# Key and query gammas folded into a second query weight, and a cross-attention kernel's opening laid out anew

## What is computed

```python
def _rms_norm(t, gamma):
    var = jnp.mean(jnp.square(t), axis=-1, keepdims=True)
    return t * jax.lax.rsqrt(var + EPS) * gamma
q = x @ Wq.T + bq                       # x: LayerNorm of x
kv = c @ Wkv.T + bkv                    # k and v interleaved
q = _rms_norm(q, q_gamma)
k = _rms_norm(k, k_gamma)
scores = jnp.einsum('bhnd,bhmd->bhnm', q, k) * scale
attn = jax.nn.softmax(scores, axis=-1)
out = jnp.einsum('bhnm,bhmd->bhnd', attn, v)
x = x + out
x = x + ffn(layernorm(x))               # 128 -> 512 -> 128, a piecewise-linear GELU, rounded to 1/256
```

## Time and profile before

| | us |
|---|---|
| median of 3 runs | 228.75 (228.58 to 230.69) |
| the profiled execution | 229.84 |
| its span, first to last instruction | 228.0 |
| PE busy (share of the span) | 181.1 (79%) |
| DVE busy | 190.6 (84%) |
| ACT busy | 146.7 (64%) |
| POOL busy | 129.8 (57%) |
| mean granted TensorE clock | 0.963 |

### The profile page before, as it was taken

One profiled execution on the slowest core, in us unless ns is written; L12 is line 12 of the kernel. 1 busy time (PEld: TensorE's weight loads), 2 busy tenths in 40 slices (PEclk: granted clock), 3 DMA queues, 4 the chain that ended last, 5 costly groups with the idle time before them and its releaser, 6 DMA issues.

```text
span 228.0 us, 8274 instructions
## 1 busy us (share of the span) xinstructions
PE 181.1 (79%) x3228; PEld 137.0 (60%) x3228; DVE 190.6 (84%) x347; ACT 146.7 (64%) x228; POOL 129.8 (57%) x175
## 2 busy tenths in 40 slices
PE   1168869888888888888898597865999999988664
PEld 0156648776676767667677455334666765665553
DVE  6878895988987888878988817879899999999993
ACT  2023745786676767676687576685777888787531
POOL 4547658478777686777876612242544555446540
PEclk9999976999999999999999999977899999999799
DMA  3341101110011101100000000000010110110103
GB/s 83 108 147 49 46 9 44 50 50 21 26 46 46 46 1 45 46 23 23 3 4 3 3 3 0 0 4 0 0 46 11 39 46 0 49 46 0 46 3 92
DMA packets 14557, 7.46 MB, mean 33 GB/s; under 512 B 1090, under 2 KB 14405, under 8 KB 14536
## 3 DMA queue, kind: packets, MB, share of 16 engines
q1 hardware_dynamic: 14120, 6.97, 10.5%
q10 hardware_dynamic: 416, 0.20, 0.3%
HBM read 5.06 MB, written 2.10 MB: 31 GB/s over the span
## 4 chain that ended last, share of the span: by engine, by line
DVE 32%; POOL 23%; issue 18%; PE 17%; ACT 5%; DVEq 2%; DMA 1%; SPq 1%; POOLq 1%; ACTq 0%
POOL y_raw L406 5%; DVE xn_all L615 4%; DVE g_hi L824 4%; POOL qk_hat L340 4%; DVE frac L817 4%; POOL rstd L318 3%; PE banks_s L1084 3%; DVE y_raw L832 3%; POOL rstd L334 3%; POOL xn L316 3%; DVE act_q L838 3%; POOL xn L321 2%; PE bank_o L1099 2%; PE g_hi L933 2%; DVE stats L604 2%
## 5 line engine op out<-in xcount | busy, mean ns | idle before, releaser
L406 POOL TENSOR_TENSOR y_raw<-g_lo,y_raw 128x1024 f32<-128x1024 f32 x15 | 35.5, 2365 | 38.2 <-DVE frac L817 37.3
L458 ACT ACTIVATE probs<-banks_s 128x512 f32<-128x512 f32 x64 | 33.0, 602 | 2.6 <-PE banks_s L974 2.1
L1099 PEld LDWEIGHTS bank_o<-w,act_q 128*128 128x128 f32 x224 | 28.7, 204 | 5.8 <-DVE act_q L838 5.1
L1084 PE MATMUL banks_s<-x2T,w 128*128 128x512 f32 x60 | 32.2, 620 | 0.0
L1099 PE MATMUL bank_o<-w,act_q 128*128 128x128 f32 x224 | 29.9, 290 | 1.0 <-DVE act_q L838 0.8
L960 PE MATMUL g_hi<-ident,parts 128*128 128x128 f16 x256 | 20.0, 222 | 9.6 <-POOL parts L347 5.8
L347 POOL TENSOR_TENSOR parts<-qk_hat,parts 128x512 f16<-128x512 f32 x16 | 18.6, 1161 | 14.3 <-DVE parts L639 14.3
L448 ACT ACTIVATE partsT<-g_hi 128x1024 f16<-128x1024 f16 x16 | 16.4, 1024 | 13.8 <-PE g_hi L960 13.7
L429 ACT ACTIVATE xcT<-bank_in 128x512 f32<-128x512 f32 x16 | 9.6, 597 | 22.9 <-PE bank_in L920 22.9
L527 ACT ACTIVATE g_hi<-seg,gelu_hi 128x1024 f32<-128x1024 f32 x16 | 17.9, 1118 | 9.3 <-DVE y_raw L832 9.3
L960 PEld LDWEIGHTS g_hi<-ident,parts 128*128 128x128 f16 x256 | 14.8, 98 | 14.0 <-issue 7.4
(11 more groups left out here) (112 smaller groups left out, 421.5 us busy)
## 6 DMA issues: line engine op xcount, KB each, us to landing
x_all<-in_x_dram SPq DMA_DIRECT2D x16, 128.0 KB, 2.3
c_in<-in_ctx_dram SPq DMA_DIRECT2D x16, 128.0 KB, 2.2
out_dram<-x_all SPq DMA_DIRECT2D x7, 256.0 KB, 2.3
w<-in_L_ffn_w_dram SPq DMA_DIRECT2D x2, 256.0 KB
out_dram<-x_all SPq DMA_DIRECT2D x2, 128.0 KB, 1.9
wkv_raw<-in_L_xattn_Wkv_dram ACTq DMA_DIRECT2D x1, 128.0 KB, 2.5
bkv_rep<-in_L_xattn_bkv_dram SPq DMA_DIRECT2D x1, 128.0 KB
wq_raw<-in_L_xattn_Wq_dram ACTq DMA_DIRECT2D x1, 64.0 KB, 2.6
```

What stands on the lines that cost most here:

```text
L406: g.tensor_tensor(y_raw[u][:], g_lo[n % 3][:], y_raw[u][:], ALU.add).then_inc(S[f"gelu{u}_done"], 1)
L458: a.activation(probs[i][:].rearrange("p t g n -> p (t g n)"), bank_s(i), ACT.Exp).then_inc(S["probs_ready"], 1)
L1084: last = t_.matmul(out, w1[:, f0:f0 + P], x2T[gr % 2][:], start=False, stop=True)
L1099: last = t_.matmul(out, act_q[u][:, c, P * t:P * t + P], w2[:, CH // UNITS * u + c, :], start=False, stop=(u == UNITS - 1 and t == GT - 1 ...
```

## The change

- `gqk` is folded into the query weights: `wqgT` is `wqT` times `gqk`, and its bias B_QG is B_Q times `gqk`. `project_qk` makes the scaled q in `bank_qk` and, with a bias and two products more, the unscaled q in the upper half of `bank_in`; `square` reads the unscaled q and k over two banks. `scale_q` is gone, and `highs` waits for `normalise`. Because `bank_in` now holds q, project_v and transpose_in wait for `square`.
- The orders of DVE's and PE's step change; `v_blk` has four copies, two of them cleared by POOL behind step -1; loops run over four steps, from 4.
- The opening: c0 ahead of the small loads, one load of bq on ACT's queue in place of four on SP's, clears in another order, the guard's bound ahead of the bias work, ln_statistics(1) ahead of the guard.
- A bias is split over three groups of rows (from 0, 32 and 64), five operations of falling height; `pick16`, one in three rows, takes the place of `ones16`.
- The feed-forward biases are scaled between steps 1 and 3 and split behind steps 12, 13 and 14.

```diff
+        B_Q, B_QG, B_K, B_1, B_2, B_END = 0, DIM, 2 * DIM, 3 * DIM, 3 * DIM + FF, 4 * DIM + FF
+        BR = 96
+        b_q = sb("b_q", [BR, DIM])
+        b_rows = sb("b_rows", [BR, B_END])
+        b_rest = sb("b_rest", [BR, B_END])
         b_parts = sb("b_parts", [P, B_END], F16)
...
-        v_blk = [sb(f"v_blk{k}", [P, 4, PAIRS, 2, VW]) for k in range(2)]
+        v_blk = [sb(f"v_blk{k}", [P, 4, PAIRS, 2, VW]) for k in range(4)]
...
+        banks_p = ps("banks_p", [P, 1536])
+        bank_in = banks_p[:, 0:512]
+        g_hi = banks_p[:, 512:1536]
+        bank_qk = banks_p[:, 512:1024]
+        bank_qkT = banks_p[:, 1024:1536].bitcast(F16)
...
+        LOOP_FROM, LOOP_TO = 4, STEPS - 4
...
             load_x(0)
-            for gg in range(2):
-                for half in range(2):
-                    at = B_Q + 64 * gg + 32 * half
-                    sp.dma_start(b_rows[:, at:at + 32].rearrange("p (i d) -> p i d", d=DH),
-                                 bq_d[64 * gg:64 * gg + 64].rearrange("(i f d) -> f i d", f=2, d=DH)[half].unsqueeze(0).to_broadcast([3, 4, DH])).then_inc(S["small_loaded"], 16)
-            for dst, src in (
-                             (bkv_rep[:], bkv_d.unsqueeze(0).to_broadcast([P, 2 * DIM])),
-                             (gq_rep[:], gq_d.unsqueeze(0).to_broadcast([P, DH])),
-                             (gk_rep[:], gk_d.unsqueeze(0).to_broadcast([P, DH]))):
+            load_c(0, 0)
+            for dst, src in ((gq_rep[:], gq_d.unsqueeze(0).to_broadcast([P, DH])),
+                             (gk_rep[:], gk_d.unsqueeze(0).to_broadcast([P, DH])),
+                             (bkv_rep[:], bkv_d.unsqueeze(0).to_broadcast([P, 2 * DIM]))):
                 sp.dma_start(dst, src).then_inc(S["small_loaded"], 16)
...
-            load_c(0, 0)
             load_x(1)
             load_c(1, 1)
             load_x(2)
             load_x(3)
...
-                             (b_rows[:, B_1:B_2], b1_d.unsqueeze(0).to_broadcast([3, FF])),
-                             (b_rows[:, B_2:B_END], b2_d.unsqueeze(0).to_broadcast([3, DIM]))):
+                             (b_rows[:, B_1:B_2], b1_d.unsqueeze(0).to_broadcast([BR, FF])),
+                             (b_rows[:, B_2:B_END], b2_d.unsqueeze(0).to_broadcast([BR, DIM]))):
                 sp.dma_start(dst, src).then_inc(S["ffw_loaded"], 16)
...
-            def scale_q(s):
-
-                wait(pool, "qk_normed", s + 1)
-                q = qk_hat[:, 0, :, :].rearrange("p t (h d) -> p (t h) d", d=DH)
-                g.tensor_tensor(q, q, gqk[:, :].unsqueeze(1).to_broadcast([P, 2 * HEADS, DH]),
-                                ALU.mult).then_inc(S["q_scaled"], 1)
-
...
-                    scale_q(s + 1)
...
-            g.memset(ones16[:], 1.0).then_inc(S["consts_ready"], 1)
-            step(-2)
-
+            g.memset(pick16[:], 0.0).then_inc(S["pick_set"], 1)
...
+            for part in range(3):
+                if part:
+                    pool.wait_ge(S["consts_ready"], part + 1)
+                g.memset(pick16[32 * part:32 * part + 1, :], 1.0).then_inc(S["consts_ready"], 1)
+            pool.wait_ge(S["consts_ready"], 4)
             g.memset(parts[:], 0.0).then_inc(S["parts_zeroed"], 1)
...
+            step(-2)
...
+            step(-1)
+            for k in range(2, 4):
+                g.memset(v_blk[k][:, :, :, :, :].rearrange("p b q h e -> p (b q h e)"), 0.0).then_inc(S["v_zeroed"], 1)
+            pool.wait_ge(S["v_zeroed"], 4)
+            for k in range(2, 4):
...
+            for s in range(0, LOOP_FROM):
...
+            act.dma_start(b_q[:], bq_d.unsqueeze(0).to_broadcast([BR, DIM])).then_inc(S["small_loaded"], 16)
...
             def square(s):
                 wait(act, "qk_proj", s + 1)
                 wait(act, "ms_ready", s)
-                a.activation(qk_sq[:].rearrange("p t q d -> p (t q d)"), bank_qk, ACT.Square).then_inc(S["qk_squared"], 1)
+                a.activation(qk_sq[:].rearrange("p w t d -> p w (t d)"),
+                             banks_p[:, 256:1280].rearrange("p (w r) -> p w r", w=2)[:, :, 0:2 * DIM], ACT.Square).then_inc(S["qk_squared"], 1)
...
-            for k in range(2):
+            v.memset(minus_max[:], 0.0).then_inc(S["g_done"], 1)
+
+            def clear_v(k):
                 v.memset(v_blk[k][:, :, :, :, :].rearrange("p b q h e -> p (b q h e)"), 0.0).then_inc(S["v_zeroed"], 1)
-            v.memset(minus_max[:], 0.0).then_inc(S["g_done"], 1)
...
-                wait(dve, "q_scaled", s + 1)
+                wait(dve, "qk_normed", s + 1)
...
-                wait(dve, "pv_done", s - 1)
+                wait(dve, "pv_done", s - 3)
+                if isinstance(s, int) and s == 2:
+                    dve.wait_ge(S["blocks_set"], 8)
...
-                    bias_v(s + 1, 1 - par)
-                    normalise(s + 1)
+                    bias_v(s + 1, (par + 1) % 4)
                 if runs(s, STEPS):
                     copy_parts(s)
                 if runs(s + 1, STEPS):
+                    normalise(s + 1)
...
+            clear_v(0)
             step(-3, 1)
+            clear_v(1)
...
                 if stage == 0:
-                    setup(v.tensor_copy(b_hi[:, cols], b_rows[:, cols]))
-                    setup(v.tensor_tensor(b_rest[:, cols], b_rows[:, cols], b_hi[:, cols], ALU.subtract))
+                    setup(v.tensor_copy(b_parts[0:BR, cols], b_rows[:, cols]))
                 elif stage == 1:
-                    setup(v.tensor_copy(b_mid[:, cols], b_rest[:, cols]))
-                    setup(v.tensor_tensor(b_rest[:, cols], b_rest[:, cols], b_mid[:, cols], ALU.subtract))
+                    setup(v.tensor_tensor(b_rest[0:64, cols], b_rows[0:64, cols], b_parts[0:64, cols], ALU.subtract))
                 elif stage == 2:
-                    setup(v.tensor_scalar(b_pick[:, cols], b_hi[:, cols], ident[0:3, 0:1], None, ALU.mult))
-                    setup(v.scalar_tensor_tensor(b_pick[:, cols], b_mid[:, cols], ident[0:3, 1:2], b_pick[:, cols], ALU.mult, ALU.add))
+                    setup(v.tensor_copy(b_parts[0:64, cols], b_rest[0:64, cols]))
+                elif stage == 3:
+                    setup(v.tensor_tensor(b_rest[0:32, cols], b_rest[0:32, cols], b_parts[0:32, cols], ALU.subtract))
                 else:
-                    v.scalar_tensor_tensor(b_parts[0:3, cols], b_rest[:, cols], ident[0:3, 2:3], b_pick[:, cols],
-                                           ALU.mult, ALU.add).then_inc(S[ready], 1)
-
-            dve.wait_ge(S["small_loaded"], 16 * 7)
-            dve.wait_ge(S["identity_ready"], 1)
+                    v.tensor_copy(b_parts[0:32, cols], b_rest[0:32, cols]).then_inc(S[ready], 1)
...
+            v.scalar_tensor_tensor(gqk[:], gq_rep[:], float(DH) ** -0.5, gk_rep[:], ALU.mult, ALU.mult).then_inc(S["gqk_ready"], 1)
...
+                v.tensor_copy(b_rows[:, at:at + 64].rearrange("p (f i d) -> p f i d", f=2, d=DH),
+                              b_q[:, 64 * gg:64 * gg + 64].rearrange("p (i f d) -> p f i d", f=2, d=DH)).then_inc(S["bq_ready"], 1)
...
+            dve.wait_ge(S["bq_ready"], 2)
+            setup(v.tensor_tensor(b_rows[:, B_QG:B_K].rearrange("p (h d) -> p h d", d=DH), b_rows[:, B_Q:B_QG].rearrange("p (h d) -> p h d", d=DH),
+                                  gqk[0:BR, :].unsqueeze(1).to_broadcast([BR, HEADS, DH]), ALU.mult), then=False)
...
+            v.tensor_tensor(wqgT[:].rearrange("p (h d) -> p h d", d=DH), wqT[:].rearrange("p (h d) -> p h d", d=DH),
+                            gqk[:].unsqueeze(1).to_broadcast([P, HEADS, DH]), ALU.mult).then_inc(S["w_ready"], 1)
+            dve.wait_ge(S["setup_dve"], done)
+            for stage in range(5):
                 bias_parts(slice(B_Q, B_1), stage, "bqk_ready")
...
+            step(-2, 2)
             guarded(dve, guard)
...
-            step(-2, 0)
-            ffn_weights()
-            step(-1, 1)
-            bias_parts(slice(B_1, B_END), 0, "ffn_ready")
-            step(0, 0)
-            bias_parts(slice(B_1, B_END), 1, "ffn_ready")
-            bias_parts(slice(B_1, B_END), 2, "ffn_ready")
-            step(1, 1)
-            bias_parts(slice(B_1, B_END), 3, "ffn_ready")
-            with dve.Fori(LOOP_FROM // 2, LOOP_TO // 2) as j:
-                step(2 * j, 0)
-                step(2 * j + 1, 1)
-            for s in range(LOOP_TO, STEPS):
-                step(s, s % 2)
+
+            ffn_bias = slice(B_1, B_END)
+            for s in range(-1, 2):
+                step(s, s % 4)
+            scale_w1()
+            step(2, 2)
+            setup(v.tensor_scalar(b_rows[:, B_1:B_2], b_rows[:, B_1:B_2], FIX, None, ALU.mult))
+            step(3, 3)
+            with dve.Fori(LOOP_FROM // 4, LOOP_TO // 4) as j:
+                for k in range(4):
+                    step(4 * j + k, k)
...
+            step(12, 0)
+            bias_parts(ffn_bias, 0, "ffn_ready")
+            step(13, 1)
+            bias_parts(ffn_bias, 1, "ffn_ready")
```

(30 more changed lines are left out.)

111 lines of the change are left out of this document (56 added, 55 removed).

## The result

| | before | after |
|---|---|---|
| median, us | 228.74 (228.58 to 230.69) | 221.68 (220.02 to 222.46) |
| the profiled execution | 229.84 | 221.93 |
| its span | 228.0 | 220.0 |

The ratio is 0.968 [0.963, 0.973]: 7.1 us less. The prediction said 218.8, range 215.3 to 223.7.

The account below looks back on a forecast made before the run. The closed chain through POOL's `scale_q` was taken as the bound. normalise(15) at 117.5 against 126.60 saves 9.1 us, 9.9 with the last `highs`; 228.75 - 9.9 = 218.85, rounded to 218.8 us, range 215.3 to 223.7.

Parts of the forecast that it names:

- The bound of before: Mid-kernel attention step: a closed chain in which `highs` waits for POOL's `scale_q`, 2.62 + 3.78 + 0.73 = 7.13 us.
- The step: Attention step after the change, `normalise` to `normalise`: 6.5 us, or 6.7 with PE at its upper bound.
- DVE's own work: VectorE's instructions in one attention step without idle time: 7.18 - 1.01, some 6.15 us, the step's lower end.
- the chain of the new order through `bias_v`: Attention step: copy_parts, normalise, highs, lows, transposes, times_v, project_v, bias_v, estimated at 6.3 us in all.
- a chain through POOL's `pow`: Attention step without scale_q, if `highs` is held till `pow` ends: 2.62 + 3.78 = 6.40 us, the likelier value.
- The hold of `highs` by `pow`: Attention step: DVE's `highs` and POOL's `pow` exclude each other, so the step is 6.40 us instead of 6.15.
- PE's term: project_qk in each of 16 steps: two products and a bias more, +0.55 us; PE's need then 6.05 to 6.7.
- Rival 1: PE becomes the bound of the attention steps, 6.7 to 6.85 us each: 221.6 to 223.7 us; chance 0.24.
- Rivals 2, 3 and 4: 2: VectorE alone, 6.15 to 6.3 (0.16). 3: clock falls, 240 (0.05 with other losses). 4: saving lost, 226 to 229 (0.05).
- The opening: Before the steady steps: bias parts ready at 10.0 us, `square` at 13.4, first `normalise` at 16.2, normalise(1) at 24.1.
- The late biases: Five feed-forward splitting operations behind steps 12 to 14, 0.8 us each; 1.6 us net ahead of normalise(15); early scaling 0.8.
- The sum: Whole kernel: normalise(15) at 24.1 + 14 x 6.5 + 0.8 + 1.6 = 117.5 us, span 218.1, median 218.8.

Follow-up runs that it names:

- the second profile: The changed kernel profiled again, unaltered, beside three other kernels on one chip: 220.35 us, 0.968 of the kernel before.

## Why the prediction held, point by point

- *The bound of before* was right in that `scale_q` put back alone brings the old wait and a step of the old length.
- *The step* was forecast at 6.5 and is 6.61 (6.55 in the second profile). The forecast had DVE's own work at 6.15, the chain of the new order through `bias_v` at 6.3 and a chain through POOL's `pow` at 6.40, held this last for the likeliest and added 0.1 for handovers. The chain that counts, beside PE, is the one at 6.3: outside the loop it measures 6.40, and that through `pow` 6.25. The prediction's sum for it was 6.26; `copy_parts` to `normalise` is 0.73 where it had 0.6, and the rest nearly fits. DVE's own work was put too low for the new order as well: the starts of `copy_parts`, `normalise` and `highs` are 0.24 us further apart than in the old one, which the prediction, costing the order at no instruction, had at nothing. The 0.1 for handovers stands where the loop costs 0.15 to 0.2, which it didn't name. So the kind of mechanism was right, which chain was not, and the closeness of 6.5 is in part luck.
- *The hold of `highs` by `pow`* isn't shown. POOL's timeline of the changed kernel has `pow` here:

```profile
64.88 0.69 POOL L328 TENSOR_TENSOR rstd<-var_eps,minus_half 128x2 f32<-128x2 f32 x1
```

  It ends at 65.57, and `highs` starts at 65.67, but also as `normalise` ends. In the kernel without loops `highs` starts 0.72 or 0.73 behind `normalise` and 0.15 after the end of `pow` (70.07 + 0.69), and the chain through `pow` is 2.63 + 3.62 = 6.25, shorter than the 6.40 of the step. The old order on DVE has `highs` start before `pow` has ended, if only by 0.1 us: in the step shown above at 64.30, with this `pow`:

```profile
63.71 0.69 POOL L328 TENSOR_TENSOR rstd<-var_eps,minus_half 128x2 f32<-128x2 f32 x1
```

  `highs` follows `copy_parts` by 0.60 and takes 0.68 all the same: no hold shows over the last tenth. An order in which `highs` starts in the middle of `pow` was not made, so that stays open. For the cast of the feed-forward bias the hold is there: 3.02 us in place of 0.47 beside POOL's clears. The Trainium skill, "SBUF — State Buffer", section "Who interferes with whom", has a VectorE cast in a two-port mode and a GpSimd instruction exclude each other, whoever is first; the 3.02 us of this cast agree with it.
- *PE's term* (+0.55 a step, need between 6.05 and 6.7) was well sized: with one more such term an ordinary step takes 7.01 to 7.07 in the loop and 6.85 ahead of it, so as it stands I estimate PE's need at about 6.5 in the loop and 6.30 ahead of it. Rival 1 gave it the bound alone; that is refuted (less PE work gives next to nothing), though PE is within 0.1 us of the bound. The time fell in rival 1's numbers (221.6 to 223.7), outside the 217.4 to 220.2 that the forecast held likeliest, but mostly by the opening and the end and not by PE.
- *Rivals 2, 3 and 4* fell: a step of 6.15 to 6.3 wasn't reached, the granted clock stayed full in the steps, and the time in hand of `square` was enough in the new order. The one that could have been lost was not listed: with project_v in its old place the same fold is 1.7% slower than before.
- *The opening* was mis-sized most: bias parts at 11.27 in place of 10.0, `square` 14.80 (13.4), `normalise(0)` 17.61 (16.2), `normalise(1)` 25.76 (24.1). The splitting itself was right, 3.3 us from `gqk` to the end. What failed is the start: the prediction let it start at about the 6.90 of before, and bkv, behind c0, landed some 1 us later. The 1.66 us at `normalise(1)` are the largest error in the span, but most of it is not the prediction's: in the second profile of the same kernel `normalise(1)` is at 24.26, 0.16 from the forecast, with bias parts at 11.13, `square` at 14.48 and `normalise(0)` at 16.85 still late. The 7.9 of the interval behind it were 8.15 and 7.41.
- *The late biases*: 0.47, 0.81, 0.48, 0.81 and 0.48, together 3.05 where 4.0 were forecast; `normalise(15)` loses 1.2 in place of 1.6, and scaling w1 and b1 costs about 0.3 in place of 0.8. From `normalise(1)` to `normalise(15)` it takes 93.1 us, forecast 93.4: less these 1.5, a step is 91.6/14 = 6.54, which is 0.6 more in all, and the biases are 0.9 less.
- *The sum*: the span was forecast at 218.1 and is 220.0: +1.66 from the opening, -0.31 from the steps, +0.55 behind them. The median lies 1.7 us above the profiled span and not 0.75, another +0.9. That is the 2.9 us between 218.8 and 221.68. The second profile has a span of 217.2, below the forecast, so errors of this size are within what executions differ by.

## What to carry to other kernels

Where one engine waits for another in every step, find the closed chain by its starts and take an instruction off it, even at the price of more work on an engine with idle time; but work out then what that engine's new need is, and which buffer the new work holds, since the same fold with one call in its old place was slower than before. When a long wait is gone, the next bound can be a closed chain whose waits, here 0.15 us a step on DVE, are too short for the list of waits, and an engine's busy time and old idle time don't give the pace: go along the chain by the starts. The order of dependent instructions added 0.24 us a step here and the loop 0.15 to 0.2. A gain in the opening is worth only what the next engine's late work leaves of it: of 4.0 us won on PE, POOL's clears took all but 0.6.

## What the runs showed of the chip that was not expected

- In the opening PE's products were 0.42 us apart; after ten idle products they were 0.22 apart, and after waits of about a microsecond 0.42 again. The granted clock shows this half rate at one time and not at another: with the products 0.42 apart it reads 1.00 in the changed kernel (12.0 to 14.5 and 20.5 to 22.0 us) and 0.51 in its second profile (19 to 21 us).
- The float16 cast of 96x640 on DVE took 0.47 us late in the kernel and 3.02 beside POOL's memory clears. The other way round, a multiplication on POOL took 1.03 us in place of 0.61 beside `highs`.
- On DVE, `normalise` behind `copy_parts` and `highs` behind `normalise` start 0.72 to 0.73 us apart, `copy_parts` behind `normalise` 0.61, with durations of 0.68 and 0.69. For `highs` it is the one instruction that reads what the one ahead has just written; why `normalise` pays it too isn't shown.
- With a loop over four steps an ordinary step takes 0.1 to 0.15 us more, and now and then one takes 0.3 to 0.9 us more than its neighbours, in two runs with PE idle for 0.8 to 0.9 and waiting on nothing that the profile shows. Written in line this goes, but the time at the ends varied by as much as that gained.
